# TensorE's order in an attention kernel: steps in fours instead of pairs, V units of two tiles

## The reference

```python
q = (layer_norm(x, ln1_w, ln1_b) @ q_w + q_b)   # 8 x 256 x 256
k = (ctx @ k_w + k_b)                           # 8 x 1601 x 256
v = (ctx @ v_w + v_b)
attn = softmax(where(mask, q k^T / sqrt(16), min))     # per head, over 1601 keys
hidden = (attn v) @ cproj_w + cproj_b + x
y = gelu(layer_norm(hidden, ln2_w, ln2_b) @ fc_w + fc_b)
return hidden + y @ proj_w + proj_b
```

## Time and profile before

| | us |
|---|---|
| median of 3 runs | 770.86 (765.46 to 772.29) |
| the profiled execution | 768.76 |
| its span | 767.0 |
| TensorE busy | 702.5 (92%) |
| ScalarE busy | 446.1 (58%) |
| VectorE busy | 371.3 (48%) |
| GpSimd busy | 120.9 (16%) |
| mean granted TensorE clock | 0.965 |

### The profile page before, as it was taken

How to read it: one execution, slowest core, us unless ns; L and a number is a source line. 1 busy time by engine, 2 the same in 40 slices (tenths; PEclk the granted TensorE clock), 3 DMA queues, 4 the chain that set the end, 5 groups by cost and what they waited for, 6 DMA issues and landing times.

```text
span 767.0 us, 16866 instructions
## 1 busy us (share of the span) xinstructions
PE 702.5 (92%) x7026; PEld 478.5 (62%) x7026; DVE 371.3 (48%) x824; ACT 446.1 (58%) x475; POOL 120.9 (16%) x90
## 2 busy tenths in 40 slices
PE   3657699899999999999999999999998978999997
PEld 3545466566656656666566566656664544597897
DVE  6643355265436534643464446534642331467663
ACT  3004366856676677567756775676566788733321
POOL 5222002200220032003201220131000600110010
PEclk9867799999999999999999999999999989999999
DMA  9787578657874788477938694878475800000000
GB/s 312 216 186 131 186 184 188 179 138 183 189 203 128 174 188 217 143 180 158 235 123 203 148 246 123 192 153 230 132 165 126 253 6 2 1 21 8 29 28 31
DMA packets 51275, 113.78 MB, mean 148 GB/s; under 512 B 7050, under 2 KB 40178, under 8 KB 49914
## 3 DMA queue, kind: packets, MB, share of 16 engines
q1 hardware_dynamic: 40700, 80.47, 44.5%
q10 hardware_dynamic: 10494, 32.17, 13.8%
HBM read 65.30 MB, written 47.06 MB: 146 GB/s over the span
## 4 chain that ended last, share of the span: by engine, by line
PE 76%; ACT 13%; DMA 5%; DVE 3%; issue 2%; ACTq 1%; DVEq 0%
PE O L1126 21%; PE S L1119 16%; ACT pr L583 11%; PE O L1056 10%; PE XB L1056 10%; PE O L1213 6%; PE S L1056 6%; DMA k_scr<-kpart 2%; DMA qst<-q_scr 2%; PE XB L1093 2%; PE XB L1153 2%; PE MB L1106 2%; DVE kpart L725 1%; DVE kpart L728 1%; DMA cols_s<-in_cols 1%
## 5 line engine op out<-in xcount | busy, mean ns | idle before, releaser
L583 ACT ACTIVATE pr<-S 128x1024 f32<-128x1024 f32 x416 | 400.6, 1024 | 188.6 <-PE S L1119 184.4
L1126 PE MATMUL O<-pr,vsl 128*17 128x256 f32 x3328 | 227.4, 388 | 1.3 <-DVE ot L790 1.3
L1119 PEld LDWEIGHTS S<-qst,kst 50*128 50x128 f32 x1664 | 117.1, 188 | 120.4 <-ACT pr L583 81.4
L1119 PE MATMUL S<-qst,kst 50*128 50x256 f32 x1664 | 171.7, 315 | 18.7 <-ACT pr L583 15.0
L1126 PEld LDWEIGHTS O<-pr,vsl 128*17 128x17 f32 x3328 | 75.3, 97 | 79.2 <-issue 17.7
L725 DVE TENSOR_SCALAR kpart<-O,cols_s 128x384 fp32r<-128x384 f32 x64 | 40.6, 635 | 120.7 <-PE O L1056 120.7
L771 DVE TENSOR_REDUCE mx<-MB 128x2 fp32r<-128x512 f32 x64 | 44.1, 690 | 79.0 <-PE MB L1106 79.0
L510 POOL CAST c_hi<-cT 128x768 fp32r<-128x768 f32 (+1 forms) x28 | 23.9, 852 | 348.0 <-DMA cT<-in_ctx_t 235.8
L1056 PE MATMUL XB<-w_hi,c_hi 128*128 128x256 f32 (+1 forms) x208 | 68.3, 328 | 2.1 <-DVE vsl L739 1.3
L739 DVE TENSOR_TENSOR vsl<-XB,rows_s 128x256 f32<-128x256 f32 (+1 forms) x104 | 43.3, 417 | 55.1 <-PE XB L1056 55.1
L1056 PE MATMUL O<-c_hi,w_hi 128*128 128x384 f32 (+1 forms) x128 | 52.6, 411 | 17.7 <-POOL c_lo L515 10.3
(11 more groups left out here) (100 smaller groups left out, 825.6 us busy)
## 6 DMA issues: line engine op xcount, KB each, us to landing
kst<-k_scr SPq DMA_DIRECT2D x59, 400.2 KB
k_scr<-kpart SPq DMA_DIRECT2D x48, 384.0 KB, 8.0
v_scr<-vsl ACTq DMA_DIRECT2D x8, 1768.0 KB, 11.9
kst<-k_scr SPq DMA_DIRECT2D x59, 200.1 KB
cT<-in_ctx_t ACTq DMA_DIRECT2D x21, 384.0 KB, 7.6
k_scr<-kpart SPq DMA_DIRECT2D x16, 449.0 KB, 7.1
q_scr<-qpart SPq DMA_DIRECT2D x16, 256.0 KB, 2.5
qst<-q_scr SPq DMA_DIRECT2D x59, 64.0 KB
```

What stands on the lines that cost most here:

```text
L583: nc.scalar.activation(pr[:, n % PBUF, :], S[:, 2 * (n % 2):2 * (n % 2) + 2, :] .rearrange("p a n -> p (a n)"), ACT.Exp).then_inc(s_.exp_d ...
L1119: last = nc.tensor.matmul(S[:, 2 * (n % 2) + g_, j * LQ:(j + 1) * LQ], kst[rows_, s, j, kt * P:(kt + 1) * P], qst[rows_, s, j, :], start=T ...
L1126: last = nc.tensor.matmul(O[32 * h:32 * h + VW, 0, 0:LQ], vsl[:, par, s, kt, h * VW:(h + 1) * VW], pr[:, n % PBUF, h * LQ:(h + 1) * LQ], s ...
```

## The change

TensorE goes through the steps in fours (13 in a batch). For four i, with n = 4i, it issues: the maxima unit, if there is one; the scores of n and n+1; the units of `XB` and then the K unit; the scores of n+2 and n+3; the values of n-2, n-1, n and n+1. In the fours 0, 3 and 10, where a slot ends inside the values, the units of `XB` stand between the values instead. `pr` holds 6 steps. V is made in 7 units, two tiles each (the last has one), which fill the whole bank `XB` and are taken with one instruction. For that the context's parts and `vsl` have other layouts. VectorE reads `KB` before `MB` for the maxima. SP's order of stores and fills follows the new tables. V's copy to DRAM goes to step 10 of its own batch, the load of the MLP weights to step 4 of the last batch, the roots of x to step 46. The head has its units in another order.

```diff
-PBUF = 4
+PBUF = 6
-PAIRS = STEPS // 2
+QUADS = STEPS // 4
-K_AT = {0: (0, 0), 2: (0, 1), 4: (0, 2), 6: (0, 3), 8: (1, 0), 10: (1, 1), 12: (1, 2), 14: (1, 3)}
-V_AT = {0: 0, 1: 1, 6: 2, 7: 3, 9: 4, 11: 5, 12: 6, 13: 7, 15: 8, 16: 9, 18: 10, 20: 11, 22: 12}
-MAX_AT = {3: (0, 2, 0), 5: (0, 2, 1), 9: (0, 3, 0), 11: (0, 3, 1),
-          15: (1, 0, 0), 17: (1, 0, 1), 21: (1, 1, 0), 23: (1, 1, 1)}
-DIV_AT = {1: SLOTS - 1, 8: 0, 14: 1, 21: 2}
-CPROJ_AT, XT_AT, Q_AT = 3, 4, 5
-YN_AT, YT_AT = 13, 16
-STRADDLE = (7, 20)
+K_AT = {0: (0, 0), 1: (0, 1), 3: (0, 2), 4: (0, 3), 5: (1, 0), 7: (1, 1), 8: (1, 2), 10: (1, 3)}
+V_AT = {0: 0, 5: 1, 6: 2, 9: 3, 10: 4, 11: 5, 12: 6}
+MAX_AT = {1: (0, 2, 0), 2: (0, 2, 1), 5: (0, 3, 0), 6: (0, 3, 1),
+          8: (1, 0, 0), 9: (1, 0, 1), 11: (1, 1, 0), 12: (1, 1, 1)}
+CPROJ_AT, XT_AT, Q_AT = 1, 2, 3
+STRADDLE = {0: 2, 3: 3, 10: 1}
+YN_AT, YT_AT = 8, 9
...
@@ SP's order
             for b in range(B):
                 first_fill(sp, b, 3)
                 if b + 1 < B:
-                    for c in range(3):
-                        store_k(b + 1, 0, c)
+                    store_k(b + 1, 0, 0)
+                    store_k(b + 1, 0, 1)
                 first_rows(b, 2)
                 if b + 1 < B:
+                    store_k(b + 1, 0, 2)
                     store_q(b + 1)
                     store_k(b + 1, 0, 3)
                     first_fill(sp, b + 1, 0)
                     store_k(b + 1, 1, 0)
-                    store_k(b + 1, 1, 1)
                 first_rows(b, 3)
                 if b + 1 < B:
+                    store_k(b + 1, 1, 1)
+                    first_fill(sp, b + 1, 1)
                     store_k(b + 1, 1, 2)
-                    first_fill(sp, b + 1, 1)
+                    first_rows(b + 1, 0)
                     store_k(b + 1, 1, 3)
-                    first_rows(b + 1, 0)
                     first_fill(sp, b + 1, 2)
                     first_rows(b + 1, 1)
@@ ScalarE's loop
-                    if n == 10 and b == 0:
-                        store_v(0)
+                    if n == 10:
+                        store_v(b)
-                    if n == 48 and b + 1 < B:
-                        store_v(b + 1)
-                    if n == 44 and b + 2 == B:
+                    if n == 4 and b + 1 == B:
                         load_mlp()
-                    if b == 0 and n == 40:
+                    if b == 0 and n == 46:
                         x_root(2 * QT, TOK, XB_VAR)
@@ TensorE
+            def v_unit(b, i):
+                bank_free(xb_taken, v_use(b, i))
+                for t, kt in enumerate(range(2 * i, min(2 * i + 2, KT))):
+                    c, m = CHUNK[kt], TAIL if kt == KT - 1 else P
+                    cut = slice(kt * P, kt * P + m)
+                    pe.wait_ge(lo_done, CH * b + c + 1)
+                    last = product3(XB[0:m, t * D:(t + 1) * D], [(c_hi[:, k, cut], c_lo[:, k, cut]) for k in range(KC)],
+                                    [(w_hi[:, 1, k, :], w_lo[:, 1, k, :]) for k in range(KC)])
+                last.then_inc(xb_ready, 1)
...
             for b in range(B):
+                for i in range(QUADS):
+                    n = 4 * i
+                    if i in MAX_AT and b + MAX_AT[i][0] < B:
+                        d, s, j = MAX_AT[i]
+                        max_unit(b + d, s, j, kb_use_max(b, i), mb_use(b, i))
+                    scores(b, n)
+                    scores(b, n + 1)
+                    if i not in STRADDLE:
+                        x_units(b, i)
+                    if i in K_AT and b + 1 < B:
+                        k_unit(b + 1, *K_AT[i])
+                    scores(b, n + 2)
+                    scores(b, n + 3)
+                    for m in range(4):
+                        if STRADDLE.get(i) == m:
+                            x_units(b, i)
+                        if n + m >= 2:
+                            values(b, n + m - 2)
+                        elif b > 0:
+                            values(b - 1, STEPS + n + m - 2)
@@ VectorE's loop
             for b in range(B):
+                for i in range(QUADS):
+                    if i in MAX_AT and b + MAX_AT[i][0] < B:
+                        d, s, j = MAX_AT[i]
+                        max_evac(b + d, s, j, kb_use_max(b, i), mb_use(b, i))
+                    if i not in STRADDLE:
+                        x_units(b, i)
+                    if i in K_AT and b + 1 < B:
+                        k_evac(b + 1, *K_AT[i])
+                    if i == 0 and b > 0:
+                        take_o(b - 1, 3)
+                    if i == 3:
                         take_o(b, 0)
...
+                    if i in STRADDLE:
+                        x_units(b, i)
+                    if i == 0 and b > 0:
+                        divide(b - 1, 3)
+                    if i == 3:
+                        divide(b, 0)
...
```

More of the change, by code:

```diff
@@ L108, in mb_pairs @@
[L108 to L133, removed]
@@ L136, in xb_use @@
[L136 to L148, removed]
-def k_use(b, mt, c):
-    return HEAD_K.index((mt, c)) if b == 0 else kb_use(b - 1, pair_of(K_AT, (mt, c)))
@@ L156, in v_use, with max_quads, k_quads, x_quads @@
[L156 to L163, removed]
+def max_quads(b):
+    return [j for j, (d, _, _) in MAX_AT.items() if b + d < B]
+def k_quads(b):
+    return list(K_AT) if b + 1 < B else []
+def x_quads(b):
+    return ([CPROJ_AT] if b > 0 else []) + ([XT_AT, Q_AT] + list(V_AT) if b + 1 < B else [])
+def uses_before(head, quads, b, j):
+    return head + sum(len(quads(i)) for i in range(b)) + sum(q < j for q in quads(b))
@@ new lines, in mb_use, with xb_use, kb_use_max, kb_use_k @@
+def mb_use(b, j):
+    return uses_before(len(HEAD_MAX), max_quads, b, j)
+def xb_use(b, j):
+    return uses_before(len(HEAD_X), x_quads, b, j)
+def kb_use_max(b, j):
+    return uses_before(len(HEAD_K), max_quads, b, j) + uses_before(0, k_quads, b, j)
+def kb_use_k(b, j):
+    return uses_before(len(HEAD_K), max_quads, b, j + 1) + uses_before(0, k_quads, b, j)
+def quad_of(table, what):
+    return [j for j, w in table.items() if w == what][0]
+XB_END, MB_END, KB_END = xb_use(B, 0), mb_use(B, 0), kb_use_max(B, 0)
@@ L652, in _ @@
                         h_root(first, 0, 0, HEAD)
-                    if b == B - 1 and n == 2 * YT_AT + 4:
+                    if b == B - 1 and n == 4 * YT_AT + 6:
                         act.wait_ge(mlpw_lo, 2)
                         y_t(first, 0)
-                    exponential(first, b, n)
+                    exponential(first, b, n, (STEPS * b + n) % PBUF)
             gelus(first)
@@ L660, in _ @@
                     for n in range(STEPS):
-                        exponential(whole, b, n)
+                        exponential(whole, b, n, n % PBUF)
                 h_root(whole, 0, 0, TOK)
@@ L973, in norms, with x_units @@
-            def norms(b, p):
-                if p == 1 and b + 1 < B:
+                v_evac(0, 1 + c)
+            max_evac(0, 0, 0, HEAD_K.index("m00"), HEAD_MAX.index("m00"))
+            v_evac(0, 5)
+            max_evac(0, 0, 1, HEAD_K.index("m01"), HEAD_MAX.index("m01"))
+            v_evac(0, 6)
+            max_evac(0, 1, 0, HEAD_K.index("m10"), HEAD_MAX.index("m10"))
+            max_evac(0, 1, 1, HEAD_K.index("m11"), HEAD_MAX.index("m11"))
+            def x_units(b, i):
+                more = b + 1 < B
+                if i in V_AT and more:
+                    v_evac(b + 1, V_AT[i])
+                if i == CPROJ_AT and b > 0:
+                    hidden(b - 1, xb_use(b, i))
+                if i == XT_AT and more:
+                    xt_evac(xb_use(b, i))
+                if i == Q_AT and more:
+                    q_evac(b + 1, xb_use(b, i))
@@ L976, in norms @@
+            def norms(b, i):
+                if i == 1 and b + 1 < B:
                     x_normalise(b + 1)
-                if b == 0 and p in XSUMS_AT:
-                    if p == 6:
+                if b == 0 and i in XSUMS_AT:
+                    if i == 3:
                         dve.wait_ge(xrest_in, 16)
-                    x_stats(XSUMS_AT[p])
-                if b == 0 and p == 18:
+                    for n in XSUMS_AT[i]:
+                        x_stats(n)
+                if b == 0 and i == 9:
@@ L999, in _ @@
                         take_o(b, 0)
-                    if p == 20:
+                    if i == 6:
+                        take_o(b, 1)
+                    if i == 10:
                         take_o(b, 2)
-                    units(b, p)
-                    if p == 13:
-                        take_o(b, 1)
-                    if p == 0 and b > 0:
-                        take_o(b - 1, 3)
-                    norms(b, p)
+                    if i in STRADDLE:
+                        x_units(b, i)
@@ L1262, in units @@
                     pe.wait_ge(mb_taken, MB_END)
[L1263 removed]
+                    pe.wait_ge(xb_taken, xb_use(b, i))
                     turn_y(first, 0)
             for b in range(B):
```

(2 more changed lines are left out.)

233 lines of the change are left out of this document (92 added, 141 removed).

## The result

| | before | changed |
|---|---|---|
| median, us | 769.9 (765.5 to 772.3) | 834.4 (823.4 to 836.7) |
| span of the profiled execution | 767.0 | 834.9 |
| mean granted TensorE clock | 0.965 | 0.911 |

The changed kernel takes 1.080 times as long, 95% interval 1.068 to 1.092. I had forecast 769 with a range to 790.

A forecast was written before the change was run, and what follows sets the result against it. TensorE's chain was taken to bound it, alternating with exponentials late in each batch. From 767.0 span: -0.5 head and batch 0, -2.5 batches 1 to 5, -4.2 batch 6, +5.4 last, giving 765.2; forecast median 769, range 752 to 790.

The forecast's parts named there:

- The floor of a four and the sum of a batch: Each four takes at least 4.82 us; 13 of them plus uncovered units make 72.5 per batch, 73.8 with waits.
- The price of a change of tiling: On TensorE, a change of tiling mode costs 0.13 to 0.21 us; four steps of values take 1.85.
- Rival (3): A group of values costs 0.44 us for its tiling change, not 0.13: faster, 737; chance 0.05.
- Term (c), the fill of slot 0: Next batch's fill lands at 46.8 us, so maxima at four 8 wait 0.8; bounds nothing and 4 us.
- Rival (1): SP's K stores and fills land one after another; a slow second fill delays the third: slower, 785; chance 0.27.
- The last batch: With hardly any units to merge, it takes 68.4 us plus 0.4, +5.4 against before; bounds +4 and +9.
- regular gaps could let it fall: Sign of being wrong: granted clock below 1 in a steady batch, TensorE's regular gaps costing more than their length.
- Batch 6 and the MLP weights: Weight load moves to step 4 of the last batch, so batch 6 falls from 78.0 to 73.8: -4.2 us.
- Batch 0: Head and batch 0, from the stop for slot 2's fill at 82.8: -0.5 us, between -4 and +4.
- The 2 us that I gave the new head: Q and K units come earlier in the new head, estimated to gain 2 us at slot 2's fill.
- The tail: After the last batch's values: the forecast's sum holds no term for a change there.

The follow-up runs named there:

- e6b: Changed kernel with context loads at steps 12 to 18, plus matmuls nobody reads in TensorE's gaps in the last batch: 777.3 us.
- e1: Changed kernel with context loads moved from steps 24, 28, 32, 36 to 12, 14, 16, 18: 789.6 us, 1.027 times before.
- e9: Changed kernel with only the maxima units of slots 2 and 0 one four later: 794.8 us.
- e8: Changed kernel with early context loads, pairs in the last batch, and maxima units of slots 2 and 0 one four later: 753.5 us, 0.982 times before.
- e2: Changed kernel loading only 16 columns of each context chunk from batch 2 on, at the old steps: 792.1 us in a single run.

## Why the prediction was wrong

**The floor of a four and the sum of a batch**: right. 4.82 was forecast and measured; four 3 with Q inside the values 6.94 and 6.87, four 5 6.08 and 6.13, fours 10 6.56 and 6.81; the batch 72.5 plus waits, 73.8, and 73.3 to 73.7 where no fill is late. The price of a change of tiling, 0.13 for a group of values, held: four steps take 1.85. Rival (3), a change of tiling at 0.44, is refuted by that row.

**Term (c), the fill of slot 0**: this step failed. I took its length, 14.1 us, from the earlier trace rows and kept it, with an upper bound of 18 from the second fill. The store and issue times were right to 1 us. But the fill moved from ScalarE's step 15 of the batch to its step 20 or 21 (by the exponentials' starts), and I never laid it beside ScalarE's queue, whose context loads stand at steps 24, 28 and 32. I noted the loads only as what slowed the second fill. Beside them, and beside the start of the second fill, the fill takes 17 to 22 us. The wait was forecast as 0.8, with a bound of 4; by the times of the four before step 32 it was 3 to 10 us in the batches 0 to 5 (from steps 28 to 32 it took 7.8 to 15.1 us, and 5.1 in batch 6). Over 5.1, the batches 0 to 5 sum to 41 us of such wait, low clock inside it included. Rival (1), the fills set the pace, had the right kind and the wrong one of them: it expected the third fill, which took 16 to 18 and cost under 1 us in most batches.

**What a wait sets off**: missing. In the wait for slot 0's fill or just behind it the granted clock fell to its half level (1.2 instead of 2.4 GHz), for 7 to 14 us in the batches 0 to 4 and for 3.4 in batch 5; I had priced that for the start of batch 0 only. In the batches 1 to 5 it takes at most about 2 us each: they are 42.9 longer than five batches of 73.3 would be, 32.1 of that are the fours with the wait, and the rest holds short waits for other fills too (2.4 us in batch 5).

**The last batch**: +5.4 forecast, +16.7 measured. The floor part is right: with its gaps filled (e6b) the batch took 69.5, and the forecast was 68.4. The missing 10 to 12 us are the clock, by the pair e1 and e6b; in e9, where it fell less often, they were 4. I had written that regular gaps could let it fall, as something that would show the forecast wrong, for a steady batch, where it did not happen, and gave it neither a price nor a chance in the last batch, where it did. A stretch with pieces at the half clock stood in the trace of before. The Trainium skill's page on the clock (TensorE: Matmul & The Clock Gate, Why this matters for your kernels) warns of long idle gaps between bursts of matmuls; here no gap was as long as 1 us in an ordinary four of the last batch, and the clock fell again and again, though not in all of such fours (e9). The measurement decides.

**Batch 6 and the MLP weights**: right, -4.2 forecast, -4.7 measured. **Batch 0**: -0.5 forecast, +13.5 measured: 8.5 of it is the fill of slot 0 again, and the other 5 were not separated (the clock is at its half level for 35 us of that batch, 14 before). With early loads (e1) it is +2.4, and with later maxima too (e8) -4.0. The 2 us that I gave the new head are 1.1: slot 2's maxima unit starts at 81.8, before at 82.9. **The tail**: no change forecast, +4.4, of which 3.5 lie between the last exponential and the MLP; the first 12 us of it ran at a granted clock of 0.85, before at 1.00.

Not settled: why the changed kernel's fill takes 17 us in some batches and 22 in others. In the batches 2 and 3 (columns 3 and 4 of the table) the three context loads leave at the same 2.7, 7.8 and 12.6 us after its first issue and the second fill 13.6 and 13.5 us after it, and the fill takes 16.6 and 21.3. No run moves the second fill alone, so its share in the length is open; with the context loads out of the way it alone did not stretch the first (e1, e2).

## What to carry to other kernels

When a step moves in an order written out by hand, lay every queue of DMAs beside its new place, not only the one it stands in: a transfer keeps its length only while its company stays the same. A fill that landed 7.6 us before it was wanted in the kernel before, and would have landed just in time in the new order (0.3 us ahead in batch 6), was the limit of this kernel as soon as 1.2 MB of loads, which nobody waited for, shared its time; moving those loads cost nothing and gave back 45 us. And an order that makes an engine wait a little in each round can have two prices, the wait and the clock that it may let fall; look at the emptiest stretch of the kernel for the second.

## What the runs showed of the hardware

Two queues of one core share the DMA engines so that 1.2 MB in the one made a 1.4 MB fill in the other 3 to 8 us longer (14 us, then 17 to 22), at a DMA share of 0.99 (batch 3). With two gaps of TensorE of 0.4 to 0.9 us in each four of 4.8 us the granted clock was at half for much of the last batch (0.75 to 0.79 in the mean of three profiles, 0.88 in e9), but it also stayed full for 27 us over such fours in e9. In steady batches without a late fill, where a unit fills the first gap, it stayed at 1.00. Matmuls that do nothing useful in those gaps made the batch 11.6 us shorter.
